# Narrow cross attention of a two-layer transformer block: steps of four heads instead of two, keys in their natural layout, softmax sums divided out behind the values

## The reference

```python
q = (x @ Wq + bq).reshape(B, Tx, 16, 16).transpose(0, 2, 1, 3)
k = (xf @ Wk + bk).reshape(B, Txf, 16, 16).transpose(0, 2, 1, 3)
v = (xf @ Wv + bv).reshape(B, Txf, 16, 16).transpose(0, 2, 1, 3)
probs = softmax(einsum('bhqd,bhkd->bhqk', q * 0.25, k), axis=-1)
out = einsum('bhqk,bhkd->bhqd', probs, v).transpose(0, 2, 1, 3).reshape(B, Tx, 256)
out = out @ Wo + bo
```

## Time and profile before

| | us |
|---|---|
| median of 3 runs (lowest, highest) | 1761.83 (1761.54, 1762.9) |
| span of the profiled execution | 1760.7 |
| stage D's preparation, 1176 to 1203 | 27 |
| stage D's loop, 1203 to 1641 | 438 |

### The profile page before, as it was taken

How to read it: one execution, slowest core, us unless ns; L and a number is a source line. 1 busy time by engine, 2 the same in 40 slices (tenths; PEclk the granted TensorE clock), 3 DMA queues, 4 the chain that set the end, 5 groups by cost and what they waited for, 6 DMA issues and landing times. The chain is left out here.

```text
span 1760.7 us, 38446 instructions
## 1 busy us (share of the span) xinstructions
PE 1636.4 (93%) x11768; PEld 1302.0 (74%) x11768; DVE 1121.2 (64%) x2767; ACT 1033.7 (59%) x2922; POOL 269.6 (15%) x504
## 2 busy tenths in 40 slices
PE   6999999979999999999999979879999999999787
PEld 4676767657887888788788868867777777777676
DVE  5656555666676667677666754455777867778543
ACT  3646463745665655556466634336878778787554
POOL 3101010132112111312211100021121111211000
PEclk9999999989999999999999989988999999999899
DMA  8000000012000000000000020000000000000000
GB/s 224 2 1 0 1 0 1 0 32 79 7 7 7 7 10 10 7 7 7 7 7 7 7 73 1 0 13 8 14 7 13 13 7 13 7 13 7 0 22 21
DMA packets 25260, 29.10 MB, mean 17 GB/s; under 512 B 1322, under 2 KB 23160, under 8 KB 24952
## 3 DMA queue, kind: packets, MB, share of 16 engines
q1 hardware_dynamic: 25208, 28.52, 5.7%
HBM read 26.68 MB, written 1.84 MB: 16 GB/s over the span
## 5 line engine op out<-in xcount | busy, mean ns | idle before, releaser
L754 ACT ACTIVATE B_probs<-bank,B_neg_max 112x375 f32<-112x375 f32 x256 | 145.0, 572 | 154.8 <-DVE B_neg_max L835 154.8
L1346 ACT ACTIVATE D_probs<-bank,D_neg_max 112x375 f32<-112x375 f32 x256 | 144.8, 571 | 76.3 <-DVE D_neg_max L1438 76.3
L835 DVE TENSOR_REDUCE B_neg_max<-bank 112x1 f32<-112x375 f32 x256 | 128.2, 542 | 94.0 <-PE bank L925 93.6
L1438 DVE TENSOR_REDUCE D_neg_max<-bank 112x1 f32<-112x375 f32 x256 | 128.0, 542 | 42.6 <-PE bank L1520 41.1
L591 PE MATMUL bank<-B_ctxT,B_wk_hi 128*128 128x378 f32 x390 | 122.9, 369 | 1.5 <-DVE B_wq_lo L824 1.5
L1353 ACT ACTIVATE D_probsT<-bank 126x336 f32<-126x336 f32 x262 | 104.3, 459 | 1.9 <-PE bank L1530 1.9
L951 PE MATMUL bank<-B_probsT,B_v 126*64 126x112 f32 x1584 | 105.0, 268 | 0.0
L843 DVE TENSOR_SCALAR B_probs<-B_probs,B_rsums 112x375 f32<-112x375 f32 x258 | 100.6, 432 | 4.6
L1446 DVE TENSOR_SCALAR D_probs<-D_probs,D_rsums 112x375 f32<-112x375 f32 x258 | 100.4, 431 | 4.6
L1544 PE MATMUL bank<-D_probsT,D_v 126*32 126x112 f32 x1584 | 101.5, 263 | 0.2 <-ACT D_probsT L1353 0.2
L935 PEld LDWEIGHTS bank<-ident,B_probs 112*126 112x126 f32 x786 | 86.7, 140 | 18.5 <-DVE B_probs L843 2.3
(11 more groups left out here) (298 smaller groups left out, 4257.2 us busy)
## 6 DMA issues: line engine op xcount, KB each, us to landing
ctx<-in_ctx_dram SPq DMA_DIRECT2D x34, 189.0 KB
ctx<-in_ctx_dram SPq DMA_DIRECT2D x34, 92.2 KB
w_stage<-in_L_xattn_Wq_dram SPq DMA_DIRECT2D x2, 1024.0 KB, 7.3
w_stage<-in_L_xattn_Wp_dram SPq DMA_DIRECT2D x1, 2048.0 KB, 8.1
w_stage<-in_L_xattn_W_dram SPq DMA_DIRECT2D x2, 1024.0 KB, 6.6
out_dram<-x_tokens SPq DMA_DIRECT2D x4, 448.0 KB, 3.2
x_tokens<-in_x_dram SPq DMA_DIRECT2D x1, 1344.0 KB, 19.7
w_stage<-in_L_xattn_Wk_dram SPq DMA_DIRECT2D x1, 1024.0 KB, 10.0
```

The costliest lines, as they stand in the source:

```text
L754: nc.scalar.activation(P[:, u % PS, j, 0:S], SB[j][0:N, 0:S], ACT.Exp, bias=nm[:, u % PS, j:j + 1], accum_out=sm[:, u % PS, j:j + 1]).then ...
L835: nc.vector.tensor_reduce(nm[:, u % PS, j:j + 1], SB[j][0:N, 0:S], AX.X, ALU.max, negate=True).then_inc(max_done, 1)
L1346: nc.scalar.activation(P[:, u % PS, j, 0:S], SB[j][0:N, 0:S], ACT.Exp, bias=nm[:, u % PS, j:j + 1], accum_out=sm[:, u % PS, j:j + 1]).then ...
L1438: nc.vector.tensor_reduce(nm[:, u % PS, j:j + 1], SB[j][0:N, 0:S], AX.X, ALU.max, negate=True).then_inc(max_done, 1)
```

## The change

PSUM becomes one tensor `banks` of eight banks, so that one instruction can read several. In stage D:

- A step has four heads (`m`, 4 steps per sequence). `scores` makes twelve products, four row tiles at once in four banks, in three passes: q_hi with k_hi, q_hi with k_lo, q_lo with k_hi. `values` makes twelve products in four column tiles at once.
- Keys stay in natural order, two blocks of 128 columns for each sequence. ACT writes k_hi with its bias straight from PSUM, one DVE instruction k_lo. The queries are laid out so that the other head's half of each slot is zero.
- The maxima are taken for two heads in one instruction. The probabilities are not divided. The transposed tiles of two heads leave in one instruction: the first half on ACT, the second on DVE; both halves use the same two banks in turn.
- The 16 sums of a sequence get one reciprocal, are spread to 32 columns each (`D_rsums_wide`), transposed by four transposes, copied out by ACT (`D_rsums_turned`) and multiplied with the values' result by one DVE instruction (`o_scaled`). V's bias stands in V's second half-slot instead.
- All projections of a sequence are made at once; the sequences of a group are unrolled in one loop; the queries of the next group are made inside the last sequence of this one. The two banks of the score tiles become four, and there is one set of them; two sets of probabilities instead of four slots.
- Stage A zeroes the bias rows on POOL before their DMAs; Wo is loaded by 16 DMAs instead of 4.

```diff
+        bv = sb("bv_rows", [ST, H, DL])
+        PT = sb("probsT", [ST, 4, NS * N])
+        oT = sb("oT", [128, MT * N])
+        rce = sb("rsums_wide", [N, H, 32])
-        SB, TB, OB, YB, PJ = k.bank[0:2], k.bank[2:4], k.bank[4], k.bank[5], k.bank[6:8]
+        SB, TB = k.psum[:, 0:4, :], k.psum[:, 4:6, :]
+        OB, PJ = k.bank[6], k.bank[7]
...
+            def pt_evac(i):
+                act.wait_ge(t_done, 2 * i + 1)
+                nc.scalar.activation(PT[:, 0:2, :], TB[0:ST, :, 0:NS * N], ACT.Copy).then_inc(pt_act, 1)
+
+            def exps(i, t, odd, m, half):
+                act.wait_ge(max_done, 2 * i + half + 1)
+                for j in range(2 * half, 2 * half + 2):
+                    nc.scalar.activation(P[:, m % 2, j, 0:S], SB[0:N, j, 0:S], ACT.Exp, bias=nm[:, m % 2, j:j + 1],
+                                         accum_out=sm[:, odd, 4 * m + j:4 * m + j + 1]).then_inc(exp_done, 1)
+
+            def keys(n, c):
+                act.wait_ge(k_mm, n + 1)
+                nc.scalar.activation(kh[:, c, :], PJ[:, 0:SP], ACT.Identity, bias=bk[:, c:c + 1]).then_inc(k_hi, 1)
+
+            def rsums(t):
+                act.wait_ge(rb_mm, t + 1)
+                nc.scalar.activation(rbs[:, :], PJ[:, 0:MT * N], ACT.Copy).then_inc(rb_out, 1)
...
+                for b in range(GB):
+                    t = g * GB + b
+                    for m in range(MT):
+                        i = 4 * t + m
+                        pt_evac(i)
+                        exps(i, t, b % 2, m, 0)
+                        if m == 0:
+                            keys(2 * t + 1, 1)
+                        if m == 2:
+                            keys(2 * t + 2, 0)
+                        exps(i, t, b % 2, m, 1)
+                        if m == 0:
+                            rsums(t)
+                            cx.act_hi(nc, act, t + 1, (TB[:, 0, :], TB[:, 1, :]))
+                        if b == 1 and m == 1:
+                            ln.act_full(nc, act, g + 1, (TB[:, 0, :], TB[:, 1, :]))
+                        if b == 3 and m % 2:
+                            queries(g + 1, m - 1, PJ)
+            pt_evac(4 * B)
+            rsums(B)
...
+            def maxima(i, m, half):
+                if half == 0:
+                    dve.wait_ge(s_done, S0 + i + 1)
+                nc.vector.tensor_reduce(nm[:, m % 2, 2 * half:2 * half + 2], SB[0:N, 2 * half:2 * half + 2, 0:S], AX.X,
+                                        ALU.max, negate=True).then_inc(max_done, 1)
+
+            def pt_evac(i):
+                dve.wait_ge(t_done, 2 * i + 2)
+                nc.vector.tensor_copy(PT[:, 2:4, :], TB[0:ST, :, 0:NS * N]).then_inc(pt_dve, 1)
...
+            def keys(n, c):
+                dve.wait_ge(k_hi, n + 1)
+                nc.vector.scalar_tensor_tensor(kl[:, c, :], PJ[:, 0:SP], bk[:, c:c + 1], f32(kh[:, c, :]), ALU.add,
+                                               ALU.subtract).then_inc(k_lo, 1)
+
+            def new_values(n, odd, s, bank):
+                dve.wait_ge(v_mm, n + 1)
+                nc.vector.tensor_copy(v[:, odd, s, :, 0, :], bank[0:ST, 0:D].rearrange("p (h d) -> p h d", d=DL)
+                                      ).then_inc(v_out, 1)
+
+            def rsums(t, odd):
+                dve.wait_ge(exp_done, EXP0 + 16 * t)
+                nc.vector.reciprocal(rc[:, :], sm[:, odd, :]).then_inc(rcp_done, 1)
+                dve.wait_ge(rcp_done, t + 1)
+                nc.vector.tensor_copy(rce[:, :, :], rc[:, :].unsqueeze(2).to_broadcast([N, H, 32])).then_inc(rce_done, 1)
+
+            def o_scaled(t):
+                dve.wait_ge(rb_out, t + 1)
+                dve.wait_ge(av_done, 4 * t + 2)
+                nc.vector.tensor_tensor(oT[:, :], OB[:, 0:MT * N], rbs[:, :], ALU.mult).then_inc(o_out, 1)
...
+                    for m in range(MT):
+                        i = 4 * t + m
+                        maxima(i, m, 0)
+                        maxima(i, m, 1)
+                        if m == 0:
+                            rsums(t, 1 - b % 2)
+                        pt_evac(i)
+                        if m == 0:
+                            keys(2 * t + 1, 1)
+                            cx.dve_lo(nc, dve, t + 1, (TB[:, 0, :], TB[:, 1, :]))
+                        if m == 1:
+                            o_scaled(t)
+                            new_values(3 * (t + 1), 1 - b % 2, 0, PJ)
+                        if m == 2:
+                            keys(2 * t + 2, 0)
+                            y_update(t)
+                            new_values(3 * (t + 1) + 1, 1 - b % 2, 1, TB[:, 0, :])
+                        if m == 3:
+                            new_values(3 * (t + 1) + 2, 1 - b % 2, 2, PJ)
+                            x_update(t)
+                        if b == 0:
+                            ln.dve_norm(nc, dve, g + 1, m)
+                        if b == 3 and m % 2:
+                            queries(g + 1, m, TB[:, 0, :])
...
+            def scores(t, m):
+                pe.wait_ge(exp_done, 16 * t + 4 * m + EXP0)
+                pe.wait_ge(ql_done, 4 * t + m + 1)
+                pe.wait_ge(k_lo, 2 * t + m // 2 + 1)
+                for p, (x, y) in enumerate(((qh, kh), (qh, kl), (ql, kh))):
+                    for j in range(4):
+                        r = slice(32 * j, 32 * j + 32)
+                        ins = nc.tensor.matmul(SB[0:N, j, 0:SP], x[r, m, :], y[r, m // 2, :], start=(p == 0),
+                                               stop=(p == 2), tile_position=(32 * j, 0))
+                ins.then_inc(s_done, 1)
+            def turn(m, half):
...
+                        ins = nc.tensor.transpose(TB[0:ST, j, s * N:(s + 1) * N],
+                                                  P[:, m % 2, 2 * half + j, ST * s:ST * (s + 1)], k.ident[0:N, 0:N])
                 ins.then_inc(t_done, 1)
...
+                    for j in range(4):
+                        h = 8 * (m // 2) + 2 * j + m % 2
+                        ins = nc.tensor.matmul(OB[32 * j:32 * j + 32, m * N:(m + 1) * N],
+                                               v[:, odd, s, h, :, :].rearrange("p r d -> p (r d)"),
+                                               PT[:, j, s * N:(s + 1) * N], start=(s == 0), stop=(s == NS - 1),
+                                               tile_position=(0, 32 * j))
                 ins.then_inc(av_done, 1)
...
+            def rsums():
+                for m in range(MT):
+                    ins = nc.tensor.transpose(PJ[:, m * N:(m + 1) * N],
+                                              rce[:, 4 * m:4 * m + 4, :].rearrange("p j r -> p (j r)"), k.ident[0:N, 0:N])
+                ins.then_inc(rb_mm, 1)
+            def project():
+                for m in range(MT):
+                    ins = nc.tensor.matmul(PJ[0:N, 0:D], oT[:, m * N:(m + 1) * N], wo[:, m, :], start=(m == 0),
+                                           stop=(m == MT - 1))
+                ins.then_inc(y_done, 1)
...
+                for b in range(GB):
+                    t, odd = g * GB + b, b % 2
+                    for m in range(MT):
+                        i = 4 * t + m
+                        pe.wait_ge(pt_act, i + PT0)
+                        pe.wait_ge(pt_dve, i + PT0)
+                        if m == 2:
+                            pe.wait_ge(o_out, t + 1)
+                            pe.wait_ge(v_out, 3 * (t + 1))
+                        values(odd if m >= 2 else 1 - odd, (m - 2) % 4)
+                        scores(t, m)
+                        if m == 1:
+                            pe.wait_ge(cx.lo_done, 2 * (t + 2))
+                        if m == 3:
+                            pe.wait_ge(v_out, 3 * (t + 1) + 2)
...
+                        turn((m - 1) % 4, 0)
+                        if m == 0:
+                            pe.wait_ge(q_act, 2 * g + 2)
+                            keys(1)
+                        if m == 1:
+                            pe.wait_ge(rb_out, t + 1)
+                            new_values(0, PJ)
...
+                            keys(0)
+                        if m == 3:
+                            pe.wait_ge(y_out, t + 1)
+                            new_values(2, PJ)
+                        pe.wait_ge(pt_act, i + PT0 + 1)
+                        turn((m - 1) % 4, 1)
+                        if m == 0:
+                            pe.wait_ge(k_lo, 2 * t + 2)
+                            pe.wait_ge(rce_done, t + 1)
+                            rsums()
+                            pe.wait_ge(pt_dve, i + PT0 + 1)
+                            cx.pe_turn(nc, pe, k, t + 1, (TB[:, 0, :], TB[:, 1, :]))
+                        if m == 2:
+                            pe.wait_ge(k_lo, 2 * t + 3)
+                            pe.wait_ge(o_out, t + 1)
+                            project()
...
+                            pe.wait_ge(pt_dve, i + PT0 + 1)
+                            new_values(1, TB[:, 0, :])
+                        if b == 1 and m == 1:
```

(65 more changed lines are left out.)

427 lines of the change are left out of this document (141 added, 286 removed).

## The result

| | us |
|---|---|
| before, median of 4 runs (lowest, highest) | 1762.37 (1761.54, 1763.4) |
| changed kernel, median of 4 runs | 1776.73 (1773.7, 1781.5) |
| ratio, 95% interval | 1.0078 (1.0059 to 1.0098) |
| span of the profiled execution, before and after | 1760.7, 1776.9 |
| first scores of stage D, before and after | 1204.84, 1201.28 |

The account below looks back on a forecast made before the run. PE's instruction stream bounded the old loop; serial waits would replace it. Four groups -8.2, start -3.8, end +8.4 sum to -3.6: 1757.1 us span, 1758.2 median; own range 1746 to 1771, whole range 1732 to 1794.

Parts of the forecast that it names:

- the loop's gain: Stage D's loop: a group takes 107.6 us against 109.65 before, so four groups give -8.2 us.
- the earlier start: Stage D's first scores at 1201.0 instead of 1204.84, as first queries get separate banks: -3.8 us.
- the longer end: Behind stage D's last step, turns, copies, values, `o_scaled` and project run with nothing beside them: +8.4 us.
- table load: ACT table load in each group of stage D, ahead of a copy PE waits for: 1.2 us a group.
- query rounds: Two double rounds of queries in each group, 24 products at 0.20 and their evacuation: 5.8 us a group.
- rival 4: Granted clock falls in PE's new gaps in the loop, 0.9 in the mean: 19 us, 1777; chance 0.04.
- Rival 3: PE's instructions come late at a group's end after branches: 0.3 to 7 us, 1759 to 1766; chance 0.04.
- chain of the plain step: In m = 3, scores, turn, ACT's copy, turn, DVE's copy and values run serially: 4.70 us for four heads.
- m = 1: Context parts hold the turn's banks until 1.3 us after scores begin; `o_scaled` goes ahead of values: 5.95 us.
- m = 0 and m = 2: Steps where PE waits for `k_lo` at 4.6, then transposes or project and values follow: 6.6 and 7.8 us.
- Rival 1: Waits in stage D's loop overlap better than drawn: a third hidden gives 33 us, 1725; chance 0.20.
- Rival 2: Slower plain step, four tiles abreast no faster than two: 70 us, 1829, or a third, 1778 to 1782; chance 0.22.

Follow-up runs that it names:

- Experiment 1: Changed kernel with 31 extra products of 64 columns a sequence on PE, placed where PE waits anyway: 1781.16 us, ratio 1.0101.
- experiments 3 to 5: Changed kernel with key block's ACT copy and `k_lo` moved ahead (1752.12 us), with `o_scaled` ahead of DVE's copy (1760.77), and with both (1739.07).
- experiment 2: Changed kernel without the query rounds in the loop, all groups using the first group's queries: 1759.4 us, ratio 0.9976.
- experiment 3: Changed kernel with the key block's ACT copy ahead of the exponentials and `k_lo` ahead of DVE's copy: 1752.12 us, ratio 0.9941.
- experiment 5: Changed kernel with key block's copy ahead of the exponentials, and `k_lo` and `o_scaled` ahead of DVE's copy: 1739.07 us, ratio 0.9867.
- experiment 8: Changed kernel with both copies of the turned probabilities cut to half their columns, the rest left stale: 1733.67 us, ratio 0.9829.
- experiments 6 and 9: PE's group loop written out in experiment 5's kernel (1738.29 us) and experiment 2's (1750.77); all four engines' loops, no last query rounds (1731.93; with fillings 1733.14, 1733.28).
- experiment 7: Changed kernel with scores and values issued for heads 0 and 1 first, then for 2 and 3: 1783.25 us, ratio 1.0128.
- experiment 9's second kernel: Experiment 5's kernel, loop written out on four engines, no last-group query rounds, twelve extra PE products ahead of m = 1 query rounds: 1733.14 us, ratio 0.9824.

## Why the prediction was wrong

The forecast was 1758.2, with the loop's gain and the earlier start nearly cancelled by the longer end. On the span it was 1757.1, and 1776.9 was measured: 19.8 us to explain.

| term | forecast | measured | difference |
|---|---|---|---|
| first scores | 1201.0 | 1201.28 | +0.3 |
| 16 sequences, undisturbed | 400.8 | 407.2 | +6.4 |
| table load, turn of the tokens | 4.8 + 1.6 | 0 + 1.1 | -5.3 |
| query rounds, undisturbed | 23.2 | 22.7 | -0.5 |
| low clock and PE late after the branch | 0 | 19.1 | +19.1 |
| end of the stage behind the last step, above before | 8.4 | 8.6 | +0.2 |

Their sum is 20.2, 0.4 off the 19.8. Without the term that was left at nothing the forecast would have been about 1 us off, partly by luck: hops that were too short (+6.4) and a table load that cost nothing (-4.8) nearly cancel.

- **The failed step is the term that was left at nothing: the granted clock.** The prediction had the mechanism as rival 4, "the granted clock falls in PE's new gaps", with 19 us and 1777, and gave it a chance of 0.04. It spoke from the earlier trace rows alone (busy 60%, clock 0.62; busy 96%, clock 1.00). After, PE is busy 75% and the clock is 0.95; it and the branch cost 19.1 us, at least 14.7 of them the clock, since the 4.4 in the m = 3 rounds can't be split. That rival 4's 19 is the same number is luck: it spread a mean clock of 0.9 over all 64 steps, while the trace has twelve dips to the lower level and the full clock between them. Experiment 1 shows the idle time as the cause by filling it; experiments 3 to 5 show it by shortening it. A price of this size should have had weight in the forecast: between a row at 60% and one at 96% nothing said that 75% was safe.
- **Rival 3 was right too, and small in this kernel.** PE is late after its branch by 2.0 to 3.9 us in experiment 2. In the changed kernel the query products cover all but 1.4 at one of three boundaries; in the other two the low clock makes the products long enough to cover it. So the 4.4 us of the m = 3 rounds are not to be split: take away one and the other shows. The Trainium skill ("Runtime: NRT & Kernel Launch", Instruction fetch mechanics) says that a taken branch to a target outside the window forces a fetch; this case's traces agree, with idle stretches of 4.89, 3.01 and 3.41 us with the branch and none of them without it.
- **The chain of the plain step was right** in its terms (0.73, 0.86, 0.71, 0.72 against 0.74, 0.86, 0.70, 0.70). The 0.18 that is missing lies in the hops: the turn to the copy took 0.83 (1390.19 to 1391.02 and 1391.81 to 1392.64) where the earlier trace rows gave 0.80, a copy to the next PE work 0.06 and 0.14. A serial chain multiplies what its links round.
- **m = 1 was 0.32 too short:** the turn, held by the context's low parts, began 1.46 us after the scores (1373.87 to 1375.33 in the same trace), not 1.3, and the same hops do the rest. m = 0 and m = 2 were right to 0.1.
- **Rival 1 (waits overlap) was wrong** as the change stands, but the overlap was there to be had: experiments 3 to 5 got 1.2 and 0.4 us a sequence by order alone. **Rival 2's** price of tiles abreast was wrong; its remark that any error counts 64 times was right. The 3.07 of the Trainium skill ("TensorE: Matmul & The Clock Gate", Part 3: Packing small matmuls), which the prediction laid on the streaming alone, would have made scores and values 0.33 longer together (rival 2's direction, not the third rival's); the trace has 0.03. As a factor for the whole it is near: twelve score products one after another at the 0.17 of the prediction's price would take 2.04 us (an estimate), and with the switch of tile shape they took 0.71, 2.9 times less.
- **The table load** cost nothing in this kernel: it stands at 1198.45, ahead of the first scores, and beside the query rounds at 1312.12, 1426.68 and 1538.29. In experiment 3 it stands at 1198.15, and the first step took 6.17 like all others, at a clock of 1.00.

Where the gain went: the change took 75 us of PE's busy time out of the stage (419 to 344). One set of score banks and one pair of turn banks put it back as waits, some 112 us of idle PE up to 1659 where there had been 19. Moving three instructions of a sequence on DVE and two on ACT took 38 us out again (experiment 5), some 27 by the order itself and the rest mostly by the clock.

## What to carry to other kernels

When an engine that was 96% busy is relieved, draw the chain through its neighbours before counting the gain: with one set of buffers every turn of a bank is on the path, and each small helper queued ahead of such a copy counts once per round. Where TensorE gets idle stretches that it did not have (here 1.3 to 1.8 us, 49 of them), price the clock by the nearest rows of the same kernel, and give it a real chance. And look at what covers a loop's branch: work that seems to be a cost of its own may be hiding it.

## What the runs showed of the hardware

- The granted clock of TensorE fell to its lower level twelve times, for some 3 to 4 us, in a loop where PE was busy 75%. Each time an idle stretch of 1.28 to 1.81 us had ended at most 1.6 us before. Of the twelve stretches of 1.68 to 1.81 us nine were followed so, of the 37 shorter ones only three; experiment 8, with none over 1.52 in the loop, had no dip there. Which round it hit, m = 1 or m = 3, changed with small edits elsewhere (experiments 6 and 9). By which rule is open.
- PE with a loop body of 2,015 recorded instructions (experiment 2) was late by 2.0 to 3.9 us after the branch back; written out, four times as long, it was not late. With 2,067 (experiment 5) 1.1 to 1.6 us showed behind the query products.
- Products in free tiles are started ahead of program order (experiment 7), so the order of issue among tiles mattered little: 0.2 us in the 24 records of the values.
- An f32 product of 64 columns with 128x128 weights took 0.22 us at the full clock (24 records in 2.67 us from 1286.13 to 1288.80, experiment 9's second kernel), twice the 0.10 that a quarter of a product of 256 columns suggests (four in 1.63 us, 1272.60 to 1274.23 in the changed kernel).
